# A two-layer kernel on one core: orders of issue changed where its stages meet, and GpSimd's feed-forward operations cut in two

## The reference, cut to what matters

```python
x = L0_attn_hidden_states                                   # [4, 512, 512]
xn = _layernorm(x)
x = x + _L0_attn_ref(xn, ...) + _L0_ffn_ref(xn, ...)        # layer 0
xn = _layernorm(x)
x = x + _L1_attn_ref(xn, ...) + _L1_ffn_ref(xn, ...)        # layer 1

# _L0_attn_ref: 32 heads of 16 features, chunks of 16 tokens, 32 steps in series
XQ, XK, XV = proj(q_w), proj(k_w), proj(v_w); eta = token_idx * sigmoid(x @ lr_w + lr_b) / HD
def step((W1, b1), (xq, xk, xv, eta)):
    Z1 = xk @ W1 + b1
    grad = layer norm's gradient at Z1 against xv - xk
    Z1_bar = xq @ W1 - eta * tril(xq @ xk.T) @ grad + b1 - tril(eta) @ grad
    W1 -= (last_eta * xk).T @ grad;  b1 -= sum(last_eta * grad)
    return xq + _ln(Z1_bar, ln_w, ln_b)
return _ln(ys, post_norm_weight, post_norm_bias) @ o_w.T

# _L0_ffn_ref: silu(x @ gate * gate_s) * (x @ up * up_s) @ down * down_s, 1408 inner features
# _L1_attn_ref: latent attention, 16 heads of 128, 4 sequences of 512
c_kv = x @ W_DKV + b_DKV; c_q = x @ W_DQ + b_DQ
k, v, q = c_kv @ W_UK + b_UK, c_kv @ W_UV + b_UV, c_q @ W_UQ + b_UQ
q[:RD], k[:RD] = rope(q @ W_QR), rope(k @ W_KR)             # half of the rotary part is zero
ctx = softmax(q @ k.T / sqrt(D)) @ v
return ctx @ W_O + b_O
# _L1_ffn_ref: 4 experts by position, silu(gate) * up, then down, 512 inner features each
```

## Time and profile before

| | |
|---|---|
| median of 3 runs | 2130.93 us (2130.27 to 2133.2) |
| profiled execution, its own time | 2132.01 us |
| its span | 2130.1 us |
| mean granted TensorE clock | 0.966 |
| busy: TensorE matmul | 1906.4 us, 89% |
| VectorE | 1208.6 us, 57% |
| ScalarE | 1009.4 us, 47% |
| GpSimd | 998.5 us, 47% |
| DMA | 297.97 MB, 41% of 16 engines |

### The profile page before, as it was taken

How to read it: one execution, slowest core, us unless ns; L and a number is a source line. 1 busy time by engine, 2 the same in 40 slices (tenths; PEclk the granted TensorE clock), 3 DMA queues, 4 the chain that set the end, 5 groups by cost and what they waited for, 6 DMA issues and landing times. The chain is left out here.

```text
span 2130.1 us, 34654 instructions
## 1 busy us (share of the span) xinstructions
PE 1906.4 (89%) x12632; PEld 1437.8 (67%) x12632; DVE 1208.6 (57%) x2367; ACT 1009.4 (47%) x2173; POOL 998.5 (47%) x765
## 2 busy tenths in 40 slices
PE   5897988899999999678999789999999999999997
PEld 3675767666666655567777567777777777777775
DVE  4662655686877764355243356555566555655552
ACT  3332646565565655466433235444444444444441
POOL 5443656455655544200233236555555555555551
PEclk9998999999999999789999889999999999999998
DMA  7875647336335432402677751222322223222211
GB/s 256 284 274 195 199 148 249 105 105 210 120 109 174 136 112 82 148 1 94 223 262 248 253 185 41 90 109 89 102 106 110 89 100 109 109 80 90 99 41 59
DMA packets 157111, 297.97 MB, mean 140 GB/s; under 512 B 20240, under 2 KB 97296, under 8 KB 150288
## 3 DMA queue, kind: packets, MB, share of 16 engines
q1 hardware_dynamic: 156944, 295.75, 41.2%
HBM read 221.52 MB, written 74.19 MB: 139 GB/s over the span
## 5 line engine op out<-in xcount | busy, mean ns | idle before, releaser
L1915 POOL TENSOR_SCALAR probs<-probs,rsum 128x512 f32<-128x512 f32 x256 | 397.5, 1569 | 362.1 <-DVE rsum L2047 362.1
L2011 ACT ACTIVATE p_tok<-bank 128x512 fp32r<-128x512 f32 x256 | 154.5, 606 | 403.4 <-PE bank L1955 403.3
L2043 DVE TENSOR_REDUCE nmax<-bank 128x1 f32<-128x512 f32 x256 | 158.9, 683 | 111.5 <-PE bank L1947 111.5
L2053 DVE TENSOR_TENSOR p_tok<-bank,p_tok 128x512 fp32r<-128x512 f32 x256 | 173.8, 681 | 22.6 <-ACT p_tok L2011 22.6
L2003 ACT ACTIVATE probs<-bank,nmax 128x512 f32<-128x512 f32 x256 | 172.2, 694 | 4.2 <-DVE nmax L2043 4.2
L60 PE MATMUL bank<-xs,ffn_w 128*128 128x512 f32 x352 | 153.4, 436 | 10.4 <-issue 8.4
L1955 PE MATMUL bank<-ident,probs 128*128 128x128 f32 x1024 | 156.6, 276 | 6.1 <-DVE p_tok L2053 5.9
L1423 POOL TENSOR_TENSOR y_pieces<-y_tok,y_pieces 128x512 fp32r<-128x512 f32 x48 | 61.6, 1298 | 208.4 <-ACT y_pieces L1635 208.4
L1955 PEld LDWEIGHTS bank<-ident,probs 128*128 128x128 f32 x1024 | 121.8, 141 | 55.3 <-issue 28.3
L1077 DVE SCALAR_TENSOR_TENSOR pt<-bank,t_mask 128x256 f32<-128x256 f32 x256 | 91.7, 414 | 101.1 <-PE bank L864 99.7
L61 PE MATMUL bank<-xs,ffn_w 128*128 128x512 f32 x352 | 138.9, 395 | 0.0
(11 more groups left out here) (271 smaller groups left out, 4906.9 us busy)
## 6 DMA issues: line engine op xcount, KB each, us to landing
ffn_w<-ffn_pieces SPq DMA_DIRECT2D x120, 512.0 KB, 3.6
uvo<-uvo_pieces SPq DMA_DIRECT2D x16, 2048.0 KB, 7.9
wq<-wq_pieces SPq DMA_DIRECT2D x16, 1536.0 KB, 6.4
ffn_pieces<-stage SPq DMA_DIRECT2D x30, 512.0 KB, 4.2
xs<-xn_pieces SPq DMA_DIRECT2D x4, 2048.0 KB, 8.4
y_tok<-in_gup SPq DMA_DIRECT2D x32, 256.0 KB, 3.1
wk<-wk_pieces SPq DMA_DIRECT2D x16, 512.0 KB, 3.6
ffn_w<-ffn_pieces SPq DMA_DIRECT2D x16, 384.0 KB, 3.5
```

Of the source, the lines that this page charges most:

```text
L1915: nc.gpsimd.tensor_scalar(probs[:, u % 8, :], probs[:, u % 8, :], rsum[:, u % 8:u % 8 + 1], None, ALU.mult).then_inc(norm_done, 1)
L2011: nc.scalar.activation(p_tok[:, Q % 2, 0, :, hh * P:(hh + 1) * P], banks[4 + u % 2][:].rearrange("p (k q) -> p k q", k=NBLK), ACT.Copy).th ...
L2043: nc.vector.tensor_reduce(nmax[:, u % 8:u % 8 + 1], banks[u % HG][:], axis=X_AXIS, op=ALU.max, negate=True).then_inc(max_done, 1)
L2053: nc.vector.tensor_tensor(p_tok[:, Q % 2, 1, :, q], banks[4 + u % 2][:].rearrange("p (k q) -> p k q", k=NBLK), p_tok[:, Q % 2, 0, :, q].bi ...
```

## The change

It has four parts, one in each stage.

*First stage.* move_rates comes behind all piece stores. The eight cst stores of the last t leave SyncE's program and are issued by ScalarE at the end of its own.

*Scan.* wx is cleared by VectorE (with a semaphore of its own), and `spread_k(0)` goes ahead of GpSimd's two remaining clears. Each of the 136 feed-forward operations on GpSimd becomes two over 256 columns; the semaphore is raised by the second.

*Middle.* All four first token transposes are made at j = S0. The square's output goes to p_hi and not to y_tok. In the preamble a block is normalised one iteration after its sums and its square. ow_hi is made on GpSimd, out_bias comes in four parts at j = -4 to -1, ow_lo in two pairs. VectorE's `scales` of z = 0 comes behind the addition to x1 from j = 0 on. The last expert's pieces are spread over i = 1, 2, 3 like the others'. In TAIL proj 5 comes before down 3.

*Attention.* For n < 3 and for p = 3 `att_jobs` gives other orders; for p < 2 the output comes before the projections in slot 1. Outputs of the last two groups have places of their own (CLOSING) and the loop is three iterations shorter. On GpSimd `rope_low` comes ahead of the norms of its iteration; on ScalarE `rope_high` stands between the second and the third exponent. The last group's weights get a buffer uvo_end, over the space of wq and wk, and are loaded when the last projection is done. The last store of y stands behind the loop.

```diff
@@ first stage, SyncE
-                            if slot == 0 and t == NTB - 1:
-                                move_rates()
-                        store_cst(t)
+                        if t < NTB - 1:
+                            store_cst(t)
+                    move_rates()
@@ first stage, end of ScalarE's program
+                    for m in range(NF):
+                        q = NF * (NTB - 1) + m
+                        act.wait_ge(cst_done, q + 1)
+                        for e in range(2):
+                            act.dma_start(cst_dram[8 * m:8 * m + 8, NTB - 1, e, :, :],
+                                          cs[:, q % NCS, e * HX:(e + 1) * HX]).then_inc(cst_out[q % NCS], 16)
@@ scan, GpSimd (the same in low and in add_down)
+            HALVES = (slice(0, TB // 2), slice(TB // 2, TB))
-                        nc.gpsimd.tensor_tensor(hid[:, q % 2, :], up_sb[:, q % 2, :], silu_g[:, q % 2, :], ALU.mult).then_inc(prod_done, 1)
+                        for h in HALVES:
+                            ins = nc.gpsimd.tensor_tensor(hid[:, q % 2, h], up_sb[:, q % 2, h], silu_g[:, q % 2, h], ALU.mult)
+                        ins.then_inc(prod_done, 1)
-                    nc.gpsimd.memset(wx[:], 0.0).then_inc(zero_done, 1)
+                    spread_k(0)
                     nc.gpsimd.memset(sg_bd[:], 0.0).then_inc(zero_done, 1)
                     nc.gpsimd.memset(grad_bd[:], 0.0).then_inc(zero_done, 1)
-                    spread_k(0)
@@ scan, VectorE
+                    nc.vector.memset(wx[:], 0.0).then_inc(wx_zero, 1)
@@ middle
-            fills = lambda e, i: [NL + PER_G * e + x for x in (FILL.get(i, ()) if e + 1 < NEXP else range(PER_G) if i == NEI - 1 else ())]
+            fills = lambda e, i: [NL + PER_G * e + x for x in (FILL.get(i, ()))]
@@ middle, GpSimd
+                    pool.wait_ge(ow_in, 16)
+                    for k in range(NF):
+                        nc.gpsimd.tensor_scalar(ow_hi[:, k, :], ow_raw[:, k, :], small[:, SM["post_w"] + k:SM["post_w"] + k + 1], None, ALU.mult)\
+                            .then_inc(owhi_done, 1)
@@ middle, TensorE
-                        b = block_at(j, 6)
-                        if b is not None:
+                        for b in range(NBLK) if j == S0 else (j + 6,) if -3 < j <= NB - 7 else ():
                             to_tokens(0, b)
-                        if j == -3:
-                            out_bias()
+                        if -4 <= j < 0:
+                            out_bias(j + 4)
@@ middle, ScalarE (the new order of the preamble)
+                        if j < -2:
+                            spread(0, j + 6)
+                            if j + 5 >= 0:
+                                normalize(0, j + 5)
+                            if j + 4 >= 0:
+                                high(0, j + 4)
+                        else:
...
@@ attention
+        uvo_end = place("uvo_end", [P, 2, HG, HID], F32R, 64)
-        LAST = NBLK * (NG - 1) + 8
+        LAST = NBLK * (NG - 1) + 5
+        CLOSING = {NQD - 3: ((1, NG - 2, 0), (3, NG - 2, 1)), NQD - 2: ((2, NG - 2, 2),),
+                   NQD: ((0, NG - 2, 3), (1, NG - 1, 0), (2, NG - 1, 1)), NQD + 1: ((0, NG - 1, 2), (1, NG - 1, 3))}
         def att_jobs(n):
             slots = [[], [], [], []]
+            if n < 3:
+                early = {-1: (0, 1, 2, 3), 0: (4, 5), 1: (6,), 2: (7,)}[n]
+                slots[0] += [("ctx", n - 1, 0)] if n >= 1 else []
+                for x, j in enumerate(early):
+                    slots[1 + x // 2].append(("proj", 1, j))
+                return slots
+            if p == 3 and G + 1 < NG:
+                return [[("proj", G + 1, 6)], [("proj", G + 1, 7)], [("ctx", n - 1, 0)], []]
             if 1 <= n <= NQD:
                 slots[0].append(("ctx", n - 1, 0))
+            if n >= 7 and p < 2 and (n - 7) // 4 < NG - 2:
+                slots[1].append(("out", (n - 7) // 4, 2 * p))
+                slots[3].append(("out", (n - 7) // 4, 2 * p + 1))
             if G + 1 < NG:
                 slots[1].append(("proj", G + 1, 2 * p))
                 slots[2].append(("proj", G + 1, 2 * p + 1))
-            if n >= 7 and p < 2 and (n - 7) // 4 < NG:
-                slots[1].append(("out", (n - 7) // 4, 2 * p))
-                slots[3].append(("out", (n - 7) // 4, 2 * p + 1))
+            for slot, a, o in CLOSING.get(n, ()):
+                slots[slot].append(("out", a, o))
@@ attention, SyncE
+                def load_uvo_end():
+                    sp.wait_ge(pj_ready, JOBS * NG)
+                    sp.dma_start(uvo_end[:].bitcast(F32), uvo_pc[NHG - 1]).then_inc(uvo_end_in, 16)
@@ attention, GpSimd
+                    if p % 2 == 1 and G + 1 < NG:
+                        rope_low(pool, G + 1, p // 2)
                     for hh in range(HG):
                         if n + 1 < NQD:
                             norm(HG * (n + 1) + hh)
-                        if hh == 1 and p % 2 == 1 and G + 1 < NG:
-                            rope_low(pool, G + 1, p // 2)
@@ attention, ScalarE
                             for x in range(HG):
                                 exponent(HG * (n + 1) + x)
-                        if hh == 1 and p % 2 == 1 and G + 1 < NG:
-                            rope_high(act, G + 1, p // 2)
+                                if x == 1 and p % 2 == 1 and G + 1 < NG:
+                                    rope_high(act, G + 1, p // 2)
```

134 lines of the change are left out of this document (80 added, 54 removed).

## The result

The changed kernel takes 2057.3 us (median of 4 runs, 2055.9 to 2059.4) against 2131.2 before (2130.3 to 2133.2); the ratio is 0.9653, 95% interval 0.9636 to 0.9669. That is 73.9 us off, and 2061 was forecast. Run a second time beside the experiments it took 2057.4 (ratio 0.9654, 0.9637 to 0.9671). The total came out nearly as forecast, but four terms of the sum were wrong by 2.8 to 8 us, two of them in sign, and the errors cancelled. That 2061 came within 4 us is in good part luck, so the terms are what is worth reading.

What follows compares the result with a forecast made beforehand. TensorE, busy 89% of the span, was taken as the bound, so only its waits, lower-clock time and stage joins could be given back. Terms summed to 69.9 us off 2132.0, less 1.1 for the median: 2061 us, range 2046 to 2084.

Steps and rivals of the forecast that it cites:

- first stage: End of the first stage: stores shared with ScalarE let the scan start earlier, 7.5 us off (4 to 8.1).
- middle's start: Start of the middle stage: transposes first, ScalarE's chain reordered, ow_hi on GpSimd; 10 us off (7 to 11).
- last expert: Last expert: spread pieces store before attention's loads, ending ScalarE's buffer wait; 15.4 us off (13 to 16).
- attention's start: First iterations of attention: early projections fill idle time, two wait for the rotary part; 2.5 us off (0 to 4).
- steady groups: Steady attention: new orders at p = 0, 1 and 3 remove waits for ctx and qk; 24.5 us off (14 to 35).
- close: End of the run: buffer uvo_end removes the 8.00 us wait for the last weights; 12 us off (9 to 14).
- the missing waits: Signs: no last-expert wait over 2 us, no 8 us wait near the end, qk and ctx under 5 us each.
- the longest L1092: Sign: VectorE's longest operation at source line L1092 would last 0.9 us.
- the new wait for an eviction: Sign: TensorE's list would show a new wait at L1246 of 4 to 8 us; over 15 refutes the forecast.
- Halves: Scan: cutting GpSimd's feed-forward operations in two shortens VectorE's holds but delays hid_lo; 2 us lost.
- halves pay fully: Rival, scan: half-long operations block half as long, waits fall by some 13 us; 2046 us, chance 0.08.
- slower rival: Rival, attention: ScalarE's rotary copy among its exponents waits for GpSimd's combine; 7.1 us late gives 2145, chance 0.02.

Runs made afterwards that it cites:

- e4: The changed kernel with the first stage's last eight cst stores issued by SyncE again and the last expert's pieces all at i = 3 again: 2071.9 us.
- e1: The changed kernel with GpSimd's 136 feed-forward operations whole again (128x512): 2064.4 us.
- e9: The changed kernel with ow_hi made by ScalarE again and the last group's weights loaded into the one buffer uvo again: 2068.5 us.
- e5: The changed kernel with the last expert's pieces all at i = 3, attention's first loads behind their stores, and ScalarE issuing four of the rates' eight loads: 2062.8 us.
- e10: The changed kernel with ScalarE's rotary copy behind the second transpose's eviction and the rates' eight loads moved into the scan: 2048.2 us.
- e8: The changed kernel with the old order at p = 3, ctx first and parts 6 and 7 after it: 2068.1 us.
- e6: The changed kernel with ScalarE's rotary copy moved from between the exponents to behind the second transpose's eviction: 2043.2 us.
- e11: Kernel e10 with GpSimd's low part whole, the product in halves and the addition in quarters: 2045.3 us.

## Why the prediction was right, and where it wasn't

The sum was 69.9 us and the spans differ by 74.3. By the table the terms were off by -2.8 (first stage), +7.7 (scan), +0.6 (middle's start), -0.9 (what lies behind it), -2.1 (last expert), -3.5 (attention's start), +6.4 (steady groups) and -1.0 (close). Of the signs that the prediction named, the first projection at 17 us, the missing waits and the longest L1092 (0.95 us) came out; the scan's start at 191 to 192 didn't, and the new wait for an eviction was 2.9 us and not 4 to 8. One sign of being wrong did show: ScalarE waits for GpSimd's combine in groups 0 and 1 (1.9 us in two waits).

**First stage, 7.5 forecast, 4.75 and 5.3 measured.** The step that failed is the duration of the rates' chain, 1.4 us to land and 4.03 to issue, taken from a trace in which nothing else was issued at that time. Beside ScalarE's stores it is 3.3 and 5.00 (e4 against the changed kernel). The rates' first store was also issued at 181.48 and not at 180.3. Of the 5.0 us of issue time moved, 3.1 were gained.

**Halves, -2 forecast, about +4 measured.** The mechanism was described rightly on both sides, the hold shorter and the second half catching the next operation, and then weighed by where the row pointed and not by a number. The mis-sized part is the delay of hid_lo: the prediction's bounds were 7 gained on sg_bd and 8 lost, and e1 shows 5.5 gained and 2.2 lost. The holds fell from 57.0 to 46.4 us, and half of that lay on the chain to sg_bd. The rival "halves pay fully" (13 us) was three times too large, by the same row. The exclusive lock of the Trainium skill ("SBUF — State Buffer", section "Who interferes with whom"), under which the one that comes second is blocked fully, fits the operations held beside whole ones (1.39 us in place of 0.42). But the whole gain doesn't follow from it: with halves the lock was met 113 times in place of 62. The table's 5.7 us for the scan contain a difference of clock as well.

**Middle's start, 10 forecast, 10.6 measured.** The size was right, but for the order of the terms it was partly luck. ScalarE's four blocks were done 10.1 us into the stage (882.77) and not 12.2, and what followed took 6.7 us and not 4 to 5: TensorE's own transposes and bias products at the lower clock, which the prediction had beside the chain and at no cost. ow_hi's cover was right, and without it 0.36 us would be lost (e9).

**Last expert, 15.4 forecast, 13.3 measured with what follows it.** The mechanism holds (e4, e5). The window behind the last rotary weights took 10.46 us and not 9.45. The 1.8 us of clock were a mistake: the first down product runs at the lower clock in both kernels (granted 0.59 before, 0.62 after).

**Attention's start, 2.5 forecast, -1.0 measured.** The step that failed is the price of ScalarE's rotary copy, which the sum has at nothing here. At the same clock, group 0 gains 1.1 by the early projections and group 1 about 1.2 at p = 3 (a gain that the prediction counts under the steady groups), and the copy takes 3.3 (e10 against the changed kernel and against the one before). The prediction named this mechanism as its slower rival and gave it 1.1 us in hand, worked out for p = 3 in a steady group. In group 1 at p = 1, with no outputs to lengthen the iteration, there was less than nothing.

**Steady groups, 24.5 forecast, 30.9 measured.** By iteration: 0.97 at p = 0 in place of 0.66, 0.67 at p = 1 in place of 0.36, 0.74 at p = 3 in place of 0.8. For p = 0 and 1 the idle of the window, 0.66 and 0.67, is all gained, and the last output's wait for its bank never shows. The remainder at p = 0 is busy time, 14.38 to 14.04, and wasn't taken apart. At p = 3 the size was right for a reason that was half of it (e8): not GpSimd's part alone, but part 7's eviction too had to come earlier. The 0.5 left there is the rotary copy (e6).

**Close, 12 forecast, 11.0 measured.** 54.75 us against 54.1 worked out: TensorE busy 46.0 against 45.7, and waits of 5.2 us in both, though not the same ones (2.6, 1.4 and 1.2). e9 puts all but 0.2 on the second buffer.

## What to carry to other kernels

Before an operation is moved in front of others on its engine, count what queues behind it there: a copy of 0.64 us among the exponents cost 0.5 us in every group, and its old place cost nothing. The releaser that a profile names is not always the cause: for qk it had ended 0.25 us before another, and for sg_bd it was VectorE or nobody where ScalarE ended last. Look which writer ended last, or move one and see. Cutting an operation that holds another engine pays on the held side and costs on its own: whole, halves and quarters gave waits of 23.1, 17.6 and 14.0 us for sg_bd and of 16.5, 18.7 and 24.6 for hid_lo. The best cut may differ from operation to operation; e11 points that way, but its total is unclear. Before a difference of a few us in one profile is read as an effect, compare the granted clock of the two stretches.

## What was not expected of the hardware

Eight small loads that SyncE issues in 4.0 us on a quiet queue take 4.75 to 6.2 beside another engine's stores (nine profiles) and 15.6 behind the scan's first loads: issue time depends on what is queued. A VectorE operation beside GpSimd's is stretched by 0.92, 0.41 or 0.18 us as GpSimd's operation lasts 1.3, 0.8 or some 0.5.
